# VectorE's attention program written out for all pairs, and a wait for each hidden block ahead of its first down product

## The chip, the cores and the metric

The kernel runs on one core of one Trainium2 chip. The metric is the device time of one execution in microseconds (us), as a median of several runs. Times in the traces are those of one profiled execution.

## The reference

Two layers, each with a token mixer and a mixture of experts, over x of 4 x 1024 tokens with 256 channels. Each layer is x = x + s * silu(m), with both branches taken from the normalised x.

```python
# layer 0: s is a linear-attention-like mixer; m is 16 experts plus a shared one
cap = int(s * 2.0 / 16)                       # 128 tokens for each expert and batch
topk_w, topk_idx = lax.top_k(scores, cap)
g = einsum('becd,efd->becf', x_tok, Wg); u = einsum('becd,efd->becf', x_tok, Wu)
h = gelu(g) * u                               # 512 hidden channels
eo = einsum('becf,edf->becd', h, Wd) * topk_w[..., None]
...
# layer 1: s is causal attention, 16 heads of 64; m is top-2 of 8 experts
sim = einsum('bhid,bhjd->bhij', q * SCALE, k); sim = where(causal_mask, neg, sim)
attn = softmax(sim); out = einsum('bhij,bhjd->bhid', attn, v)
return out.transpose(0, 2, 1, 3).reshape(b, n, INNER) @ Wo
```

The change touches how two of these parts are ordered: layer 0's 16 experts and layer 1's attention. What is computed stays the same.

## The kernel before

The kernel is written with one program for each engine; they wait for each other by semaphores. Its stages, in order of time: normalisation and layer 0's mixer with the shared expert (to about 395 us), the 16 experts (`experts`, about 400 to 762 us) with layer 1's normalisation behind them (`renormalize`, to about 865 us), attention (`attention`, to about 2140 us) and layer 1's experts (`moe`, to the end).

**Experts.** Of each expert, 128 tokens of each of the B = 4 batches are held as 512 columns. TensorE's program of one expert is `expert` (L1026 to L1043): for each of KF = 4 blocks f of 128 hidden channels it makes gate and up (2 products of 128x512 each, L1033); it then transposes the next expert's gathered rows (`follow`, 8 transposes, L1022); and then come the down products (L1040), 4 row blocks b with 4 products each for f = 0 to 3. The listing runs `follow` and then waits for `eo_done` (the last expert's results were read) and for `hid_done` to reach 4 (e + 1): all four hidden blocks of this expert. The trace has two matmuls for each product of the listing (so 32 down matmuls and 32 of gate and up an expert) and one for each transpose. ScalarE makes the gelu of each block (L1064), VectorE multiplies it by the up half and reports it in `hid_done` (L1088), VectorE scales the results (L1093), GpSimd scatters them with addition (L993) and gathers rows for an expert 4 ahead (L973), and SyncE loads the weights two experts ahead once the down products are done (L939 to L941). Experts 0 to 11 run in a loop of 4 on TensorE, experts 12 to 15 are written out.

**Attention.** There are 4 batches (nb) with 8 pairs of heads (PAIRS), 32 pairs in all. TensorE, ScalarE and VectorE each go through one order of events for a pair, written out by hand as PE_ORDER, ACT_ORDER and DVE_ORDER; a "+" marks work of the next pair. Of VectorE's, M is the mask reduction (adds the mask to a piece of scores and takes the running maximum, L1634), I the reciprocal of the sums (L1641), A the copy of v (L1647), P the rotary products (L1654), and W adds a pair's projected output to y (L1669). TensorE's A0, A1, A4, A5 are the query and key products (L1394), A2, A3, A6, A7 the value products (L1400), S the scores (L1409), T transposes (L1417), V the products with v (L1431), W the output projection (L1441). ScalarE's E is the exponential (L1462). GpSimd adds the two halves of the rotary embedding (L1497).

`run` (L1225 to L1243) lays an engine's events out over the pairs. It writes out "first" (the work ahead of pair 0), pairs 0 and 1, then has a loop of two pairs for the rest of batch 0 (L1231), a nested loop of two pairs for batches 1 and 2 (L1234, L1235), a loop of two pairs for the first six of batch 3 (L1239), and pairs 30 and 31 written out. In a loop the values that semaphores are waited for depend on the counter and are worked out with register instructions ahead of the wait. `act_on(part, it, pr, u, seq)` gets the pair's number `it`, its number in the batch `pr`, its parity `u` and its batch `seq`.

Of the kernel before, what the change touches and what calls it, by code (L numbers as in the profile page):

```python
# [26 lines left out]
ONE = 1  # L27
# [3 lines left out]
KF = F0 // P  # L31
# [3 lines left out]
PAIRS = HEADS // 2  # L35
# [875 lines left out]
def experts(nc, d):  # L911


    with ExitStack() as ctx:
# [14 lines left out]
        t_ps, xt_done, ffn_ps, gel_done, hid_done, dn_ps, eo_done = (s.sem(x) for x in ("t_ps", "xt_done", "ffn_ps", "gel_done", "hid_done", "dn_ps", "eo_done"))  # L929
# [5 lines left out]
        with nc.Block() as block:  # L935
# [77 lines left out]
            @block.tensor  # L1013
            def _(pe):
                def turn(i, q):

                    e = i * AHEAD + q
                    pe.wait_ge(gathered[q], 16 * B * (i + 1))
                    pe.wait_ge(xt_done, KC * e + ONE)
                    for c in range(KC):  # L1020
                        for b in range(B):
                            last = pe.transpose(ps[c][:, b * P:(b + 1) * P], xg[q][:, b * C + c * P:b * C + (c + 1) * P], ident[:, :])  # L1022
                        last.then_inc(t_ps, 1)

                def expert(i, q, follow):
                    e, u = i * AHEAD + q, q % 2  # L1026
                    pe.wait_ge(xt_done, KC * (e + 1) + ONE)
                    pe.wait_ge(w_in[u], 48 * (i * 2 + q // 2 + 1) + ONE)
                    for f in range(KF):
                        pe.wait_ge(hid_done, KF * e + max(f - 1, 0) + ONE)  # L1030
                        for w, bank in ((wg[u], ps[2 + 2 * (f % 2)]), (wu[u], ps[3 + 2 * (f % 2)])):
                            for k in range(KC):
                                last = pe.matmul(bank, w[:, k * F0 + f * P:k * F0 + (f + 1) * P], xT[u][k][:, :], start=k == 0, stop=k == KC - 1)  # L1033
                        last.then_inc(ffn_ps, 1)
                    follow()
                    pe.wait_ge(eo_done, B * e + ONE)
                    pe.wait_ge(hid_done, KF * (e + 1) + ONE)
                    for b in range(B):
                        for f in range(KF):
                            last = pe.matmul(ps[6 + b // 2][:, (b % 2) * C:(b % 2 + 1) * C], hid[f][:, b * P:(b + 1) * P],  # L1040
                                             wd[u][:, f * C:(f + 1) * C], start=f == 0, stop=f == KF - 1)
                        if b % 2:
                            last.then_inc(dn_ps, 1)  # L1043

                turn(0, 0)
                with pe.Fori(0, ROUNDS - 1) as i:
                    for q in range(AHEAD):
                        expert(i, q, lambda: turn(i + (q + 1) // AHEAD, (q + 1) % AHEAD))
                for q in range(AHEAD - 1):
                    expert(ROUNDS - 1, q, lambda: turn(ROUNDS - 1, q + 1))  # L1050
                expert(ROUNDS - 1, AHEAD - 1, lambda: None)
                then["tensor"](pe)

# [106 lines left out]
def attention(nc, d, name, b0, nb, scatter):  # L1160

    with ExitStack() as ctx:
# [16 lines left out]
        def scratch(cols):  # L1179
            nonlocal at  # L1180
            at += cols
            return d.moe_w2[:, at - cols:at]

        before, bias, rank, tile_no = d.at_route
        sc, bi, w_r, tmp, slot, both, tot, run_, line = d.sc, *(scratch(W) for i in range(8))
# [39 lines left out]
        def run(eng, act_on):  # L1225

            act_on("first", -1, -1, 1, -1)
            if nb > 1:
                for u in range(2):
                    act_on("both", u, u, u, 0)  # L1230
                with eng.Fori(1, PAIRS // 2) as i:  # L1231
                    for u in range(2):
                        act_on("both", i * 2 + u, i * 2 + u, u, 0)
                with eng.Fori(1, nb - 1) as b:  # L1234
                    with eng.Fori(0, PAIRS // 2) as i:  # L1235
                        for u in range(2):
                            act_on("both", b * PAIRS + (i * 2 + u), i * 2 + u, u, b)
            it = (nb - 1) * PAIRS
            with eng.Fori(0, PAIRS // 2 - 1) as i:  # L1239
                for u in range(2):  # L1240
                    act_on("both", i * 2 + (it + u), i * 2 + u, u, nb - 1)
            act_on("both", it + PAIRS - 2, PAIRS - 2, 0, nb - 1)
            act_on("last", it + PAIRS - 1, PAIRS - 1, 1, nb - 1)  # L1243

        s.start()
        with nc.Block() as block:
# [295 lines left out]
            def _(dve):  # L1542
# [126 lines left out]
                                dve.scalar_tensor_tensor(out=part_y, in0=bank[:, t * C:(t + 1) * C], scalar=inv[:, unit:unit + 1], in1=part_y,  # L1669
                                                         op0=ALU.mult, op1=ALU.add).then_inc(w_added, 1)  # L1670

                run(dve, act_on)
                dve.wait_ge(w_added, nb * (16 * PAIRS) + 16 + ONE)


# [399 lines left out]
```

## Time and profile before

| | us |
| --- | --- |
| median of 3 runs (2583.3 to 2585.82) | 2585.6 |
| the profiled execution | 2586.59 |
| its span in the trace | 2584.8 |
| TensorE busy (matmul) | 2430.4 |
| VectorE busy | 1330.7 |
| ScalarE busy | 1104.8 |
| GpSimd busy | 554.0 |

The profile comes from one execution. PE is TensorE, PEld its weight loads, DVE is VectorE, ACT is ScalarE, POOL is GpSimd, SP is SyncE, which issues most DMAs. Instructions of an engine's sequencer (waits, register work, branches) are not counted as busy. An idle time is put down to the engine whose instruction ended it; "issue" stands where the profile shows no such instruction. The chain of waits that the page follows back from the end stays in the last stage, which the change does not touch, so it is of no use here. The granted clock of TensorE was 1.00 in the stages that the change touches, apart from short stretches.

### The profile page before, as it was taken

The numbers are of one execution on the slowest core, as the hardware profiler recorded it, in microseconds if no ns is written. First come the engines' busy times: TensorE is split into PE (matmuls) and PEld (weight loads), VectorE is DVE, ScalarE is ACT, GpSimd is POOL, SyncE is SP. The second block draws the span as 40 slices with busy tenths as digits, with TensorE's granted clock in tenths as the row PEclk, the third lists the DMA queues.
The fourth block names the chain that finished last, engine by engine and source line by source line (L and its number), as shares of the span: only waits on it lengthen the run. The fifth ranks groups of instructions, "written<-read, shape, count | busy, mean of one in ns | idle before, by whom it ended". The sixth has DMA issues, their size and how long they took to land. (4 is left out here: it accounts for less than half of the span.)

```text
span 2584.8 us, 47040 instructions
## 1 busy us (share of the span) xinstructions
PE 2430.4 (94%) x14584; PEld 1699.0 (66%) x14585; DVE 1330.7 (51%) x3699; ACT 1104.8 (43%) x2581; POOL 554.0 (21%) x510
## 2 busy tenths in 40 slices
PE   6999998999975899999999999999999999999993
PEld 5555555555545566666666666666666668999992
DVE  6766241221217866666666656666666653333334
ACT  3211111111115466666656666566666662222222
POOL 3002001444426233332111111111111101111113
PEclk9999998999998999999999999999999999999996
DMA  6013103865436323332111121111211116666696
GB/s 209 17 49 114 49 17 115 260 209 158 114 71 223 89 88 103 96 91 74 42 41 41 49 57 41 41 41 49 72 54 47 51 52 233 243 236 237 240 340 225
DMA packets 145386, 295.90 MB, mean 114 GB/s; under 512 B 16768, under 2 KB 102288, under 8 KB 134896
## 3 DMA queue, kind: packets, MB, share of 16 engines
q1 hardware_dynamic: 124320, 251.59, 30.4%
q0 software_dynamic: 20944, 42.94, 6.1%
q8 instruction: 45, 0.74, 0.1%
q14 instruction: 77, 0.63, 0.1%
HBM read 193.80 MB, written 67.12 MB: 101 GB/s over the span
## 5 line engine op out<-in xcount | busy, mean ns | idle before, releaser
L1462 ACT ACTIVATE at_p<-at_p,at_nmax 128x640 f32<-128x640 f32 (+7 forms) x512 | 392.8, 768 | 209.2 <-DVE at_nmax L1634 205.8
L1634 DVE CUSTOM_DVE_ANT_0 at_p<-at_ps,atk_mask 128x512 f32<-128x512 f32 (+3 forms) x512 | 282.9, 585 | 174.6 <-PE at_ps L1409 152.7
L1497 POOL TENSOR_TENSOR kept_big<-kept_xg 128x1024 f32<-128x1024 f32 x64 | 150.9, 2358 | 998.3 <-DVE kept_xg L1654 998.3
L1469 ACT ACTIVATE at_pT<-at_ps 128x512 f32<-128x512 f32 (+1 forms) x640 | 311.2, 574 | 100.9 <-PE at_ps L1417 100.8
L1417 PEld LDWEIGHTS at_ps<-kept_ident,at_p 128*128 128x128 f32 x2304 | 256.0, 141 | 117.9 <-issue 62.7
L1417 PE MATMUL at_ps<-kept_ident,at_p 128*128 128x128 f32 x2304 | 304.6, 277 | 15.6 <-ACT at_p L1462 15.0
L1409 PE MATMUL at_ps<-kept_big 64*128 64x512 f32 (+3 forms) x1536 | 297.2, 505 | 5.1 <-DVE at_nmax L1634 2.6
L1431 PE MATMUL at_ps<-at_pT,at_v 128*64 128x256 f32 (+1 forms) x2560 | 270.2, 362 | 1.2 <-issue 1.2
L1669 DVE SCALAR_TENSOR_TENSOR kept_big<-at_ps,at_inv,kept_big 128x256 f32<-128x256 f32 x512 | 213.9, 475 | 79.2 <-PE at_ps L1441 73.5
L1431 PEld LDWEIGHTS at_ps<-at_pT,at_v 128*64 128x64 f32 x2560 | 173.6, 137 | 115.4 <-issue 35.1
L1394 PE MATMUL at_ps<-atk_h,atk_w 128*128 128x512 f32 x512 | 238.1, 598 | 6.5 <-SPq L1256 6.5
L1033 PE MATMUL ex_ps<-kept_big 128*128 128x512 f32 x512 | 225.4, 599 | 0.9 <-ACT kept_big L1059 0.9
L1807 PEld LDWEIGHTS moe_ps<-moe_xT,moe_w 128*128 128x128 f32 x1696 | 197.6, 192 | 3.4 <-ACT moe_xT L1840 0.7
L1807 PE MATMUL moe_ps<-moe_xT,moe_w 128*128 128x128 f32 x1696 | 198.0, 275 | 0.5 <-ACT moe_xT L1840 0.5
L1409 PEld LDWEIGHTS at_ps<-kept_big 64*128 64x128 f32 x1536 | 128.1, 188 | 77.0 <-issue 39.7
L1033 PEld LDWEIGHTS ex_ps<-kept_big 128*128 128x128 f32 x512 | 98.3, 192 | 118.7 <-issue 117.9
L1064 ACT ACTIVATE kept_big<-ex_ps 128x512 f32<-128x512 f32 x64 | 38.2, 597 | 299.9 <-PE ex_ps L1033 299.9
L1782 POOL DMA_INDIRECT z_rows<-moe_yo,moe_to x71 | 68.8, 969 | 376.7 <-DVE moe_yo L1873 376.7
L1394 PEld LDWEIGHTS at_ps<-atk_h,atk_w 128*128 128x128 f32 x512 | 91.1, 193 | 85.3 <-issue 78.5
L1634 DVE CUSTOM_DVE_ANT_0 at_p<-at_ps,atk_mask,at_nmax 128x128 f32<-128x128 f32 (+3 forms) x256 | 134.9, 546 | 20.7 <-PE at_ps L1409 20.7
L1654 DVE TENSOR_TENSOR kept_xg<-kept_xg,atk_cos 128x1024 f32<-128x1024 f32 x64 | 78.1, 1220 | 128.3 <-DMA kept_xg<-kept_xg 128.3
L1088 DVE TENSOR_TENSOR kept_big<-kept_big,ex_ps 128x512 f32<-128x512 f32 x64 | 44.1, 689 | 185.6 <-ACT kept_big L1064 185.6
(236 smaller groups left out, 3349.0 us busy)
## 6 DMA issues: line engine op xcount, KB each, us to landing
moe_w<-in_w_w SPq DMA_DIRECT2D x53, 1028.0 KB, 4.8
kept_xg<-kept_xg SPq DMA_DIRECT2D x256, 128.0 KB, 2.4
atk_first_w<-in_w_w SPq DMA_DIRECT2D x18, 1028.0 KB, 4.8
atk_w<-in_w_qkv SPq DMA_DIRECT2D x32, 384.0 KB, 3.0
slot_in<-kept_big SPq DMA_DIRECT2D x9, 1032.0 KB
kept_big<-in_w_eg SPq DMA_DIRECT2D x16, 512.0 KB, 3.5
kept_big<-in_w_eu SPq DMA_DIRECT2D x16, 512.0 KB, 5.0
kept_big<-in_w_ed SPq DMA_DIRECT2D x16, 512.0 KB, 6.8
```

The source lines that it names most:

```text
L1033: last = pe.matmul(bank, w[:, k * F0 + f * P:k * F0 + (f + 1) * P], xT[u][k][:, :], start=k == 0, stop=k == KC - 1)
L1394: last = pe.matmul(banks[0], w[x][:, k * QKV + m * P:k * QKV + (m + 1) * P], h[:, k * T + half * CH:k * T + (half + 1) * CH], start=k == 0 ...
L1409: pe.matmul(banks[e][:, 0:to - at], qkT[x][e * DH:(e + 1) * DH, n * P:(n + 1) * P], qkT[x][e * DH:(e + 1) * DH, T + at:T + to], start=True ...
L1417: last = pe.transpose(banks[0][:, (i - 4 * j) * P:(i - 4 * j + 1) * P], p[(2 * t + e) % LAG][:, k * P:(k + 1) * P], ident[:, :])
L1431: last = pe.matmul(banks[0][e * DH:(e + 1) * DH, skip:QW], v[x][:, (k * 2 + e) * DH:(k * 2 + e + 1) * DH], pT[n][:, at + skip:at + QW], st ...
L1462: act.activation(buf, buf, ACT.Exp, bias=nmax[:, unit:unit + 1], scale=-1.0, accum_out=rsum[:, unit:unit + 1]).then_inc(exp_done, 1)
L1469: act.activation(dst, ring[RING_BANK[part][ev]][:, 0:(i1 - i0) * P].rearrange("p (k c) -> p k c", c=P), ACT.Copy).then_inc(t_read, 1)
L1497: pool.tensor_tensor(out=qkT[x][:, :].rearrange("p (m t) -> p m t", m=2)[:, :, half * CH:(half + 1) * CH], in0=raw[half][:, :].rearrange(" ...
L1634: ins = dve.tensor_tensor_reduce(out=p[unit % LAG][:, at:to], in0=ring[RING_BANK[part]["S", ((t, c), e), ahead]][:, 0:to - at], in1=mask[: ...
L1654: dve.tensor_tensor(out=both, in0=both, in1=table[:, half * CH:(half + 1) * CH].unsqueeze(1).to_broadcast([P, 2, CH]), op=ALU.mult).then_i ...
L1669: dve.scalar_tensor_tensor(out=part_y, in0=bank[:, t * C:(t + 1) * C], scalar=inv[:, unit:unit + 1], in1=part_y, op0=ALU.mult, op1=ALU.add ...
L1807: last = pe.matmul(bank[:, m * P:(m + 1) * P], w1[q][:, at:at + P], xT[u][:, k * P:(k + 1) * P], start=k == 0, stop=k == KC - 1)
```

## The change

TensorE, in `expert`: in place of one wait for all four hidden blocks ahead of the down products, the first row block (b = 0) waits ahead of each product f for block f alone. The other three row blocks have no wait. VectorE, in `attention`: `run(dve, act_on)` is replaced by "first" and a Python loop over all 32 pairs, so that each pair is written out with constants, and there is no loop on VectorE. Order and content of its events are the same. The programs of the other engines in attention still come from `run`.

```diff
--- before.py
+++ after.py
@@ -1034,9 +1034,10 @@
                         last.then_inc(ffn_ps, 1)
                     follow()
                     pe.wait_ge(eo_done, B * e + ONE)
-                    pe.wait_ge(hid_done, KF * (e + 1) + ONE)
                     for b in range(B):
                         for f in range(KF):
+                            if b == 0:
+                                pe.wait_ge(hid_done, KF * e + f + 1 + ONE)
                             last = pe.matmul(ps[6 + b // 2][:, (b % 2) * C:(b % 2 + 1) * C], hid[f][:, b * P:(b + 1) * P],
                                              wd[u][:, f * C:(f + 1) * C], start=f == 0, stop=f == KF - 1)
                         if b % 2:
@@ -1669,7 +1670,10 @@
                                 dve.scalar_tensor_tensor(out=part_y, in0=bank[:, t * C:(t + 1) * C], scalar=inv[:, unit:unit + 1], in1=part_y,
                                                          op0=ALU.mult, op1=ALU.add).then_inc(w_added, 1)
 
-                run(dve, act_on)
+                pairs = nb * PAIRS
+                act_on("first", -1, -1, 1, -1)
+                for it in range(pairs):
+                    act_on("both" if it < pairs - 1 else "last", it, it % PAIRS, it % 2, it // PAIRS)
                 dve.wait_ge(w_added, nb * (16 * PAIRS) + 16 + ONE)
```

## Rows read from the trace of the kernel before

**Rows 1.** The page: the engines' busy times.

```profile
PE 2430.4 (94%) x14584; PEld 1699.0 (66%) x14585; DVE 1330.7 (51%) x3699; ACT 1104.8 (43%) x2581; POOL 554.0 (21%) x510
```

**Rows 2.** Stages: us, busy us (instructions) of PE PEld DVE ACT POOL, granted clock, DMA share, GB/s.

```profile
900.00:1190.00 290.00, 290.00 (x2058) 196.54 (x2056) 185.98 (x557) 185.77 (x443) 104.23 (x97) 1.00 0.32 96
1190.00:1840.00 650.00, 640.45 (x4535) 432.26 (x4534) 410.89 (x1235) 410.23 (x969) 83.67 (x37) 1.00 0.18 47
1840.00:2060.00 220.00, 220.00 (x1574) 149.94 (x1574) 142.19 (x422) 141.73 (x336) 28.24 (x12) 1.00 0.20 53
```

**Rows 3.** VectorE's mask reductions as a group, 1190:1840, then 1840:2062.

```profile
L1634 DVE CUSTOM_DVE_ANT_0 at_p<-at_ps,atk_mask 128x512 f32<-128x512 f32 (+3 forms) x259 | 143.5, 586 | 103.4 <-PE at_ps L1409 83.4 <-issue 18.9
...
L1634 DVE CUSTOM_DVE_ANT_0 at_p<-at_ps,atk_mask 128x512 f32<-128x512 f32 (+3 forms) x88 | 48.2, 579 | 25.2 <-PE at_ps L1409 24.8
```

**Rows 4.** VectorE's timeline, a turn of the nested loop: start, length, idle before in brackets.

```profile
1257.59 3.23 DVE L1669 SCALAR_TENSOR_TENSOR kept_big<-at_ps,at_inv,kept_big 128x256 f32<-128x256 f32 x8 [1.89 <-PE at_ps L1441]
1263.48 0.56 DVE L1634 CUSTOM_DVE_ANT_0 at_p<-at_ps,atk_mask 128x384 f32<-128x384 f32 x1 [2.66 <-issue]
```

**Rows 5.** VectorE's timeline, a turn of the plain loop.

```profile
1103.41 0.56 DVE L1634 CUSTOM_DVE_ANT_0 at_p<-at_ps,atk_mask 128x384 f32<-128x384 f32 x1
```

**Rows 6.** Instruction packets of queue 14, in 880:1010, 1025:1190 and 1190:1840.

```profile
q14 instruction: 7, 0.06, 0.1%
...
q14 instruction: 1, 0.01, 0.0%
...
q14 instruction: 40, 0.33, 0.2%
```

**Rows 7.** TensorE's timeline behind the late mask reduction.

```profile
1267.42 1.09 PE L1417 MATMUL at_ps<-kept_ident,at_p 128*128 128x128 f32 x8 [1.02 <-ACT at_p L1462]
```

**Rows 8.** TensorE's timeline: where four of the pairs begin their query products.

```profile
906.35 0.59 PE L1394 MATMUL at_ps<-atk_h,atk_w 128*128 128x512 f32 x1
...
945.69 0.59 PE L1394 MATMUL at_ps<-atk_h,atk_w 128*128 128x512 f32 x1
...
1221.12 1.45 PE L1394 MATMUL at_ps<-atk_h,atk_w 128*128 128x512 f32 x3
...
1825.74 1.02 PE L1394 MATMUL at_ps<-atk_h,atk_w 128*128 128x512 f32 x2
```

**Rows 9.** TensorE's timeline, the fifth expert.

```profile
497.71 10.03 PE L1033 MATMUL ex_ps<-kept_big 128*128 128x512 f32 x23
507.58 1.04 PE L1022 MATMUL ex_ps<-kept_ident,kept_xg 128*128 128x128 f32 x8
509.15 7.17 PE L1040 MATMUL ex_ps<-kept_big 128*128 128x256 f32 x32 [0.53 <-DVE kept_big L1088]
```

**Rows 10.** VectorE's timeline in the same expert: the fourth block.

```profile
508.41 0.69 DVE L1088 TENSOR_TENSOR kept_big<-kept_big,ex_ps 128x512 f32<-128x512 f32 x1 [2.75 <-ACT kept_big L1064]
```

**Rows 11.** TensorE's waits through all experts, 398 to 770 us.

```profile
PE ex_ps L1040 <- DVE kept_big L1088: 9.8, 16, 1.5
```

**Rows 12.** TensorE's timeline: first down matmuls of the fifth, 13th and last expert.

```profile
509.15 1.35 PE L1040 MATMUL ex_ps<-kept_big 128*128 128x256 f32 x5 [0.53 <-DVE kept_big L1088]
...
687.77 1.10 PE L1040 MATMUL ex_ps<-kept_big 128*128 128x256 f32 x4 [0.63 <-DVE kept_big L1088]
...
754.91 1.32 PE L1040 MATMUL ex_ps<-kept_big 128*128 128x256 f32 x5 [1.50 <-DVE kept_big L1088]
```

**Rows 13.** GpSimd's waits, 398 to 765 us.

```profile
POOL z_rows L993 <- DVE ahead_eo L1093: 88.8, 8, 15.2
```

**Rows 14.** DMA issues in the experts, 398:765: KB each, median us to landing.

```profile
kept_big<-in_w_ed SPq DMA_DIRECT2D x14, 512.0 KB, 6.8
```

**Rows 15.** TensorE's timeline after the last expert.

```profile
784.79 0.47 PE L500 MATMUL ex_ps<-kept_ident,kept_big 128*128 128x128 f32 x1 [22.73 <-DVE kept_big L432]
```

**Rows 16.** VectorE's waits without a releaser, 880 to 1190 us.

```profile
DVE kept_big L1669 <- issue: 3.6, 2, 2.0
DVE at_p L1634 <- issue: 0.7, 3, 0.4
```

## The prediction

> **What bounds the kernel now.** I read the page's busy times first: TensorE is busy for 2430.4 of 2584.8 us [rows 1]. A change can pay only where it shortens TensorE's own queue or ends one of its waits, so each half of the change is read in its own stretch.
>
> **Attention.** The busy times by stage show TensorE without a gap from 900 to 1190 us and from 1840 to 2060 us, but 9.55 us short in the 650 us between [rows 2]. That middle stretch holds the pairs of batches 1 and 2, which run in the nested loop. Among VectorE's groups there, idle time that names no other engine stands once: 18.9 us of the mask reduction's idle time; in the same group between 1840 and 2062 us, where the pairs of batch 3 run in a plain loop of the same body, it is absent [rows 3]. VectorE's timeline shows the place: the last additions of the odd pair end at 1260.82 us, and the first mask reduction of the next pair starts at 1263.48, after 2.66 us without a releaser [rows 4]. At 1103.41 us, where batch 0's loop turns, it starts without idle time [rows 5]. The nested loop turns back seven times (three inner turns in each of two batches, and one outer turn), and seven times 2.7 us is 18.9. All three loops hold two pairs, yet only the nested one stops.
>
> What stops it is seen in the instruction packets: queue 14 brought 40 of them in the 650 us of the nested loop and one in the 165 us before [rows 6]. So I read a stop as code fetched again. The Trainium skill (Runtime: NRT & Kernel Launch, Instruction fetch mechanics) says that a taken branch whose target lies outside the buffered pages waits for a fetch; the packets agree, though at 8 KB each (0.33 MB in 40) and not the 16 KiB that it names. It has the crossing of a page in straight code mostly hidden, which is what the forecast takes.
>
> Does TensorE pay? Behind the late mask it waits 1.02 us for ScalarE's exponential [rows 7]. Its starts give the whole price. The query products of a pair begin at 906.35, 945.69 and so on every 39.35 us: (1221.12 - 906.35) / 8 = 39.35, over one pair written out on VectorE and seven looped ones. From 1221.12 to 1825.74 there are 15 pairs in 604.62 us, against 15 x 39.35 = 590.2: **14.4 us lost**, 2.05 a turn [rows 8]. The 9.55 us above are less because a matmul's modelled length covers part of each gap.
>
> **What the change does to attention.** VectorE's loops go. The 32 pairs had 10 written-out bodies and now have 32, so 22 more bodies lie in memory, and register work in front of its waits goes. TensorE, ScalarE, SyncE and GpSimd keep their programs.
> - The seven stops: 7 x 2.05 = 14.4 us, all on TensorE's path.
> - The register work is worth nothing: the pair from 906.35 to 945.69 us is already written out on VectorE and takes the same 39.34 us as the looped ones [rows 8]. Its cover is TensorE's own work; without that it would matter.
> - New fetches of straight code: the stretch from 880 to 1010 us, where pairs 0 and 1 and the first pass of the plain loop run code for the first time, drew 7 packets in 130 us [rows 6], about 2.1 a pair for all that this queue serves, and TensorE kept 39.35 us. I take 0; the other end of the bound is a rival below.
> - After a stop has gone, TensorE itself is next: from 900 to 1190 us it has no gap [rows 2].
>
> **What the change does in the experts.** Each of 16 experts ends its gate and up products, turns the next expert's rows (8 transposes) and then waits for the fourth hidden block. In TensorE's timeline the transposes start at 507.58 and are 0.11 apart, so the eighth starts at 508.35 and a product could follow at 508.46; the first down product starts at 509.15 [rows 9], since VectorE's fourth product runs from 508.41 to 509.10 [rows 10]. The waits sum this as 9.8 us in 16 [rows 11], of which the last expert, without transposes, has 1.50 and the 13th 0.63 [rows 12].
>
> Now the products on blocks 0 to 2 of the first row block may start before the fourth block is there; the third was ready one block earlier, 8 matmuls of 0.43 or 3.4 us. Each product is two matmuls in the trace (32 an expert for 16 in the listing). The 32 take 7.17 us; less 0.38 for the last one's length and 0.1 for the first one's exposed weight load, 31 steps make 0.216 each [rows 9]. The exposed load is read from the first five: 1.35 us, where four steps and one length make 1.24 [rows 12]. Three products are 6 x 0.216 = 1.30 us, more than the 0.64 us from 508.46 to 509.10. So the fourth never waits: an expert gains the whole gap of 0.69 and the 0.11 of the load, 0.80. For the 13th to 15th it is 0.1 more, and for the last one, whose products could start after the last up matmul but whose gap is longer than 1.30, it is 1.30. **12 x 0.80 + 3 x 0.90 + 1.30 = 13.6 us.** Below, the bound is 0; above, this is all the idle time there is.
>
> The added waits, three more an expert, I take at nothing: in the gate and up part a wait on the same semaphore already stands ahead of each block, with a value worked out from the loop counter, and 23 matmuls still take 10.03 us without a gap, 0.43 each [rows 9]. That work is the cover, and here it is 0.22 a matmul. If it is gone, the nearest row is the 13th expert's idle time of 0.63 against 0.53 in the loop [rows 9, 12], so 0.1 a wait, 48 x 0.1 = 4.8 us given back. The Trainium skill (Advanced Engine Details and Errata, Network/Comms) puts the reading of a semaphore at 50 to 100 ns. By estimate that is 2.4 to 4.8 us for the 48 and speaks against this edit; no row shows such a cost where matmuls are queued.
>
> Behind the waiting products stand only down products of the same expert. VectorE's scaling and GpSimd's scatter wait for them and come earlier too. GpSimd idles some 10 us an expert before its scatter (8 waits make 88.8 us) [rows 13] and keeps up with a period of 21.5 instead of 22.3 us. The weights for the expert after next are asked for as the next expert begins and needed a period later; the last of them land in 6.8 us [rows 14]. What follows the last expert hangs on its scatter, its rows read back and normalised: TensorE waits 22.73 us for that [rows 15], so the 13.6 us are handed on whole.
>
> **Sum.** The profiled execution took 2586.6 us (span 2584.8 and 1.8 around it), 1.0 above the median of 2585.6. 2586.6 - 14.4 - 13.6 = 2558.6; against the median, **2557.6 us**.
>
> **Rivals.**
> 1. *The early products gain little*, because added waits hold TensorE's queue up: with nothing gained 2585.6 - 14.4 = 2571.2 us, with 4.8 us given back of the 13.6, 2562.4. For it: their cover halves. Against it: the gate and up part. The skill's 50 to 100 ns would end between 2560.0 and 2562.4.
> 2. *The turn still costs*, since TensorE's and ScalarE's loops turn at the same pairs, or another cause sits there: only the experts pay, 2572.0 us. Against it: both loops also turn in batch 0, at 39.35 us a pair.
> 3. *Slower: straight code stops at the ends of its pages.* A stop at the loop's end costs 2.05 us. If each written-out pair had one such stop ahead of a mask reduction, 31 x 2.05 = 63.6, less 28.0, is 35.6 more: 2621.2 us. It decides from 28.0 / 2.05 = 14 stops on. Against it: in batch 0 VectorE has only 0.7 us of waits without a releaser before mask reductions in 310 us [rows 16], though its first two pairs are written out. It has 3.6 us more before its last additions; a looped pair idles there too, 1.89 us, for TensorE [rows 4], so I take these for TensorE's product.
> 4. *Nothing measurable changes*: another limit (a read-back, a row gather) takes both gains: 2585.6 us.
>
> **How the numbers follow.** The forecast has 0.68, with 2554 to 2561 as its own range; rival 1 has 0.15, rival 2 0.08, rival 3 0.05, rival 4 0.04. The predicted time is the likeliest case's. The range for 8 in 10 takes in the forecast and rival 1, with the runs' spread of 1 to 2 us (2583.3 to 2585.8): 2553 to 2572 us. A measurement can tell about 0.2%, or 5.2 us. Faster by more: 0.68 + 0.15 + 0.08 = 0.91. Within it: 0.04. Slower: 0.05.
>
> **What would show it.** In the profile after, the seven nameless waits of VectorE are gone, and 15 pairs take 590 us from start to start. TensorE's wait before the down products is gone, and each looped expert takes 21.5 us. Instruction packets come steadily. The forecast is wrong if pairs run longer than 39.35 us, if nameless waits stand before mask reductions in many pairs, or if the experts' period stays at 22.3 us.

## The result and the profile after

The changed kernel takes **2559.1 us** (median of 4 runs, 2555.9 to 2560.1) against 2585.0 for the kernel before beside it (4 runs, 2583.3 to 2585.8): a ratio of 0.9896, 95% interval 0.9884 to 0.9907. The forecast of 2557.6 us, its sign and its two gains hold. The profiled execution took 2560.1 us, with a span of 2557.7, so 27.1 us of span have gone. In the listing after, the lines behind L1034 stand one lower: the mask reduction is L1635, the query products are L1395, the down products L1041.

The page's busy times of the changed kernel, to set beside [rows 1]:

```profile
PE 2421.2 (95%) x14584; PEld 1698.3 (66%) x14585; DVE 1328.0 (52%) x3699; ACT 1104.5 (43%) x2581; POOL 553.9 (22%) x510
```

TensorE's timeline after: the query products of six pairs (the stretch that answers to [rows 8]), the first of all ahead of them.

```profile
825.60 1.19 PE L1395 MATMUL at_ps<-atk_h,atk_w 128*128 128x512 f32 x1 [6.56 <-SPq L1257]
...
893.20 0.59 PE L1395 MATMUL at_ps<-atk_h,atk_w 128*128 128x512 f32 x1
...
932.54 0.59 PE L1395 MATMUL at_ps<-atk_h,atk_w 128*128 128x512 f32 x1
...
1168.62 0.59 PE L1395 MATMUL at_ps<-atk_h,atk_w 128*128 128x512 f32 x1
...
1208.59 0.59 PE L1395 MATMUL at_ps<-atk_h,atk_w 128*128 128x512 f32 x1
...
1798.85 0.59 PE L1395 MATMUL at_ps<-atk_h,atk_w 128*128 128x512 f32 x1
...
2034.93 0.59 PE L1395 MATMUL at_ps<-atk_h,atk_w 128*128 128x512 f32 x1
```

From 1208.59 to 1798.85 us there are 15 pairs in 590.26 us, where the kernel before took 604.62 [rows 8]: 14.36 us less. From the third pair on every pair now takes 39.34 to 39.42 us, but for one: 1168.62 to 1208.59 is 39.97. The stages from 893.20 to 2034.93, 1141.73 us, took 1155.47 before (906.35 to 2061.82). The busy times by stage say the same (columns as in [rows 2]):

```profile
887.00:1176.00 289.00, 289.00 (x2052) 196.29 (x2050) 184.16 (x555) 185.53 (x441) 103.72 (x96) 1.00 0.32 95
1176.00:1815.00 639.00, 638.47 (x4547) 433.84 (x4544) 412.35 (x1241) 410.93 (x972) 84.17 (x38) 1.00 0.19 48
1815.00:2033.00 218.00, 218.00 (x1568) 148.81 (x1567) 139.41 (x418) 140.85 (x333) 28.23 (x12) 1.00 0.20 53
```

TensorE is 0.53 us short of full in the middle stage, where it was 9.55 short before [rows 2]. VectorE's timeline at the place of the old stop [rows 4], first addition and first mask reduction of the pair after:

```profile
1245.04 3.23 DVE L1670 SCALAR_TENSOR_TENSOR kept_big<-at_ps,at_inv,kept_big 128x256 f32<-128x256 f32 x8 [2.00 <-issue]
1248.18 0.55 DVE L1635 CUSTOM_DVE_ANT_0 at_p<-at_ps,atk_mask 128x384 f32<-128x384 f32 x1
```

The 2.66 us ahead of the mask reduction are gone. The 2.00 us ahead of the additions are no new stop: in this stage the additions' idle time is 38.2 us in both kernels, but 32.0 of it now stands without a name, where before all of it was put down to TensorE's products. In the same stage the costliest group of mask reductions keeps one nameless wait, and queue 14 brings 15 instruction packets in the 639 us instead of 40 in 650 [rows 3, 6]:

```profile
L1635 DVE CUSTOM_DVE_ANT_0 at_p<-at_ps,atk_mask 128x512 f32<-128x512 f32 (+3 forms) x260 | 143.6, 587 | 72.5 <-PE at_ps L1410 69.5 <-issue 2.3 <-remote 0.6
```

```profile
q14 instruction: 15, 0.12, 0.1%
```

In the experts, TensorE's timeline of one expert after (the stretch that answers to [rows 9]):

```profile
482.78 1.04 PE L1022 MATMUL ex_ps<-kept_ident,kept_xg 128*128 128x128 f32 x8
483.66 7.07 PE L1041 MATMUL ex_ps<-kept_big 128*128 128x256 f32 x32
490.56 10.89 PE L1033 MATMUL ex_ps<-kept_big 128*128 128x512 f32 x25
```

The down products follow the transposes at once, and their 32 matmuls take 7.07 us where they took 7.17. The period is 21.52 us (462.14, 483.66 and 505.17 are three starts in a row). TensorE's waits from 398 to 760 us no longer hold the row of [rows 11]; these two are all that is left:

```profile
PE ex_ps L1022 <- PEq L102: 8.3, 1, 8.3
PE ex_ps L1033 <- ACT kept_big L1060: 0.9, 1, 0.9
```

The whole difference of the spans: the first query products come at 825.60 instead of 839.52 us (-13.92); from there to the third pair it takes 67.60 instead of 66.83 (+0.77); the pairs up to the last one's start -13.74; the rest 522.77 instead of 522.98 (-0.21). The sum is -27.10.

### The profile page after: what moved, and what is told of

Read it like the earlier page. It is cut to its first block and busy times, and to the rows that moved or that the text cites. A ratio compares the mean times of both kernels' runs of the same rounds, so it can differ in the third digit from the quotient of the medians.

```text
span 2557.7 us, 45455 instructions
## 1 busy us (share of the span) xinstructions
PE 2421.2 (95%) x14584; PEld 1698.3 (66%) x14585; DVE 1328.0 (52%) x3699; ACT 1104.5 (43%) x2581; POOL 553.9 (22%) x510
## 5 line engine op out<-in xcount | busy, mean ns | idle before, releaser
L1635 DVE CUSTOM_DVE_ANT_0 at_p<-at_ps,atk_mask 128x512 f32<-128x512 f32 (+3 forms) x512 | 281.8, 585 | 138.2 <-PE at_ps L1410 134.9
L1395 PE MATMUL at_ps<-atk_h,atk_w 128*128 128x512 f32 x512 | 238.0, 598 | 6.6 <-SPq L1257 6.6
L1065 ACT ACTIVATE kept_big<-ex_ps 128x512 f32<-128x512 f32 x64 | 38.2, 597 | 287.6 <-PE ex_ps L1033 276.2
L1635 DVE CUSTOM_DVE_ANT_0 at_p<-at_ps,atk_mask,at_nmax 128x128 f32<-128x128 f32 (+3 forms) x256 | 135.0, 546 | 27.5 <-PE at_ps L1410 27.1
L1395 PEld LDWEIGHTS at_ps<-atk_h,atk_w 128*128 128x128 f32 x512 | 90.8, 192 | 85.3 <-issue 78.5
```

The source lines that it names most:

```text
L1395: last = pe.matmul(banks[0], w[x][:, k * QKV + m * P:k * QKV + (m + 1) * P], h[:, k * T + half * CH:k * T + (half + 1) * CH], start=k == 0 ...
L1635: ins = dve.tensor_tensor_reduce(out=p[unit % LAG][:, at:to], in0=ring[RING_BANK[part]["S", ((t, c), e), ahead]][:, 0:to - at], in1=mask[: ...
```

## The experiments

All were timed beside the kernel before, whose medians lie between 2584.6 and 2584.7 us. A ratio is against it.

**1. The VectorE half alone.** The kernel before with the second hunk of the change:

```diff
-                run(dve, act_on)
+                pairs = nb * PAIRS
+                act_on("first", -1, -1, 1, -1)
+                for it in range(pairs):
+                    act_on("both" if it < pairs - 1 else "last", it, it % PAIRS, it % 2, it // PAIRS)
```

> Half of the change alone: VectorE's attention is written out for all pairs, the experts are as before. My theory (the seven stops at the nested loop's turns are VectorE's, and nothing else sits there): 14.4 us less than before, a ratio of 0.9944, TensorE's pairs 39.35 us from start to start throughout, no idle time of VectorE without a releaser at the old turns. The changed kernel's trace lost 0.6 us in pair 8; if that belongs to the new code it comes again here, and the gain is 13.8. The rival (the turns of TensorE's or ScalarE's own loops cost as much): less than 5 us gained.

Measured: 2573.2 us, ratio 0.9957 (0.9943 to 0.9970). In its trace the pairs from 905.88 to 2047.25 us take 1141.37 us, 14.1 less than before. This half is worth 11.5 us by the medians and 14.3 by the spans of the two profiled executions; the profiled execution of before lay 1.9 us above these runs' median. The expected 14.4 us (0.9944) stand at the edge of the interval, so it is the trace that decides, not the medians. The time outside the span was longer too: 2.3 to 2.5 us in each of these runs, 1.7 to 1.9 in those of the kernel before.

**2. The TensorE half alone.** The kernel before with the first hunk:

```diff
-                    pe.wait_ge(hid_done, KF * (e + 1) + ONE)
...
+                            if b == 0:
+                                pe.wait_ge(hid_done, KF * e + f + 1 + ONE)
```

> The other half alone: the waits for each hidden block in the experts, attention from the loops as before. My theory: 13.6 us less (12 x 0.80 + 3 x 0.90 + 1.30), a ratio of 0.9947, each looped expert 21.52 us, no idle time of TensorE before the down products, and the seven stops of VectorE still there at 2.05 us each. If the two halves shared something (a transfer or a read-back that both meet), the two gains would not add up to the whole 25.9 us; I expect them to, within 1.5 us. The rival that waits cost TensorE something has at most 8.8 us gained.

Measured: 2569.8 us, ratio 0.9945 (0.9932 to 0.9959). VectorE's waits from 1176 to 1815 us, where the nested loop is still there:

```profile
DVE at_p L1635 <- PE at_ps L1410: 89.1, 62, 3.8
...
DVE at_p L1635 <- issue: 19.1, 7, 2.9
```

Seven nameless waits of 19.1 us, as in the kernel before (18.9). So the halves are separate: 11.5 and 14.9 us by the medians, 26.4 together, and the whole change gives 25.9.

**3. Only the first product early.** The changed kernel, whose second product already waits for all four blocks:

```diff
-                            if b == 0:
-                                pe.wait_ge(hid_done, KF * e + f + 1 + ONE)
+                            if b == 0 and f < 2:
+                                pe.wait_ge(hid_done, KF * e + (1, KF)[f] + ONE)
```

> The changed kernel, but only the product on hidden block 0 may start early: ahead of the second product TensorE waits for all four blocks. Theory of the forecast (an expert gains the time that products ahead of the wait fill, up to the whole gap of 0.69 us and 0.11 for the exposed weight load): one product is two matmuls of 0.216 us, so 0.43 us an expert go ahead and the load is exposed again at the second product: 16 x 0.43 = 6.9 us of the 13.9 stay, and the time is 7.0 us above the changed kernel, 19.0 below the kernel before. TensorE then idles about 0.26 us before the second product. The rival that the gain comes from somewhere else than the overlap (from a shorter wait instruction, for instance) expects the changed kernel's time.

Measured: 2565.8 us, ratio 0.9928 (0.9915 to 0.9942), 18.9 us faster than before. TensorE's timeline of one expert in it:

```profile
485.06 7.44 PE L1041 MATMUL ex_ps<-kept_big 128*128 128x256 f32 x32
```

The products start behind the transposes, but stretch over 7.44 us instead of 7.07: the rest of the wait stands inside them. The down products begin every 21.88 us: 0.44 less than the 22.32 before, where 0.43 were expected, and 0.36 more than with the whole change. The gain goes by how much work stands ahead of the last block, as the forecast had it.

**4. Many more waits.** The changed kernel with the wait ahead of all 16 products of an expert instead of the first four, 192 waits more:

```diff
-                            if b == 0:
-                                pe.wait_ge(hid_done, KF * e + f + 1 + ONE)
+                            pe.wait_ge(hid_done, KF * e + f + 1 + ONE)
```

> The changed kernel with a wait for the hidden block ahead of each of the 16 down products of an expert instead of the first 4. All added ones are already fulfilled when they are reached. It is four times the suspected cost: 192 waits more. The forecast took an added wait at nothing behind queued matmuls: the changed kernel's time within 1 us, experts of 21.52 us. The rival of 0.1 us a wait: 19.2 us slower than the changed kernel.

Measured: 2559.5 us, ratio 0.9903 (0.9888 to 0.9918). That is 0.4 us from the changed kernel, inside either one's scatter. From the first expert's first down product to the last expert's it takes 321.86 us in both traces (335.03 in the kernel before), so the 192 waits cost nothing that a trace can show. They are there: the condition on the hidden blocks stands at 240 of the down products' weight loads, where the changed kernel has it at 48. But they are no instructions of their own (both profiles list 45455): each rides on a weight load. Waits of this kind, on a value long reached, carried by a weight load and with matmuls queued, are free on TensorE. What a wait costs as an instruction of its own is not tested here.

**5. ScalarE's program written out as well.** The changed kernel with ScalarE's `run(act, act_on)` replaced in the same manner.

> The changed kernel with ScalarE's attention program written out for all 32 pairs too. In the changed kernel's trace the pair from 1168.62 us took 39.97 us instead of 39.35, with TensorE waiting 0.53 us for ScalarE's exponential, just after ScalarE's program left its first loop and went into new code. If that is ScalarE's code being fetched late, the pair takes 39.35 us here and the time is 0.6 us less. If it was TensorE's or VectorE's, it stays. In either case ScalarE's own turns cost nothing in the other pairs, so no more than 0.7 us is to be had; straight code on two engines that stopped at its block ends would show as longer pairs.

Measured: 2559.1 us, ratio 0.9897 (0.9882 to 0.9913). Nothing is gained and nothing lost, though queue 14 brings 69 packets instead of 57. ScalarE's loops turned at no cost to TensorE. The pair expected at 39.35 us takes 39.35, but so it does in experiments 3 and 4, where ScalarE still loops, so this does not show where the 0.6 us came from.

**6 and 7. Code moved by empty instructions: failed.** The kernel before with 64 (then 128) empty instructions on VectorE ahead of attention's normalisation:

```diff
+        for _ in range(64):
+            dve.nop()
```

> The kernel before with all its loops; 64 instructions that do nothing are put into VectorE's program ahead of layer 1's normalisation, where it idles some 11 us. They move the code of all three attention loops by 64 places. Theory A, where the code lies decides: a loop body of two pairs is some 325 instructions; the code comes in packets of 8 KB, 128 instructions if one has 64 bytes; a body that touches three such blocks stays in the buffer and one that touches four does not. In the kernel before only the nested loop touches four. Moved by half a block it touches three, and the loops of batches 0 and 3 touch four: the stops move from the nested loop (7) to two turns in each of the plain loops (4), at about 1024, 1103, 1904 and 1983 us. The time falls by 3 x 2.05 = 6.2 us. Theory B, nesting or the register work in it causes the stop: seven stops where they were, no change of time.

> The control for the run with 64: another 64 instructions that do nothing stand at the start of the experts' part of VectorE's program, so the attention code is moved by 128 places, a whole block. Theory A: everything lies as before against the blocks, so the seven stops are back in the nested loop and the time is that of the kernel before, within 1 us. Theory B: the same time as well. If the extra instructions themselves cost something, it shows here as a longer time.

Measured: 2586.7 (ratio 1.0007, 0.9998 to 1.0016) and 2585.1 us (1.0003, 0.9994 to 1.0012). Both profiles list 47040 instructions, as many as before: the empty instructions never came into the program. These two are further runs of the kernel before and say nothing on the question, though the 128 case looks as if it had met its expectation.

**8 to 11. Code moved by real instructions.** The filler is now an increment of a semaphore that nobody waits for, `dve.sem_inc(d.pad, 1)`. The listings differ in their number and place alone:

```diff
+    d.pad = s.sem("pad")
...
+        for _ in range(64):
+            dve.sem_inc(d.pad, 1)
```

The question is why the nested loop stopped while the two plain loops, with the same body, didn't. Between two turns the trace lists 324 to 328 instructions of VectorE. By estimate from the order of VectorE's compiled instructions, in blocks of 128, the body of batch 0's loop begins about 1 instruction into a block, the nested one's about 73, and batch 3's about 20. A body of 325 that begins up to 59 into a block touches three blocks, and a later one touches four. The counts in the trace alone put the nested body 71 and batch 3's 143 instructions behind batch 0's, within 4 of these places. Where batch 0's body begins stands in no trace; the runs bound it, since its turns are free with 56 more instructions and stop with 64 more.

> The kernel before with 64 instructions more on VectorE, each an increment of a semaphore that nobody waits for, ahead of attention's normalisation, so that all of its loops' code moves by 64 instructions. Place theory (a loop's turn stops where its body, 325 instructions long, lies unluckily against the 8 KB blocks in which queue 14 brings code): the nested loop's seven stops go, and the plain loops of batch 0 and batch 3, two turns each, stop in their stead near 1024, 1104, 1904 and 1983 us: 3 x 2.05 = 6.2 us faster than before, 2579 us. Nesting theory (the stop belongs to the nested loop's own branches and register work): all seven stops stay where they are, no change, 2585 us.

> The kernel before with 128 instructions more on VectorE ahead of attention's loops (64 at the start of the experts' part, 64 ahead of attention's normalisation): 128 is what one packet of 8 KB holds at 64 bytes each. Both theories: the seven stops of the nested loop stay, the plain loops have none, the time is that of before, 2585 us. If the place matters but not by blocks of 128 instructions, this kernel has another number of stops than seven.

> As the kernel with 64 more instructions, but with 56. Place theory: the nested loop's seven stops go, batch 0's loop just escapes, and the two turns of batch 3's loop stop (near 1904 and 1983 us): 5 x 2.05 = 10.3 us faster than before, 2575 us. Nesting theory: seven stops stay, 2585 us.

> With 112 instructions more (56 at the start of the experts' part, 56 ahead of attention's normalisation). Place theory: the nested loop's seven stops go, batch 3's loop keeps turning without one, and the two turns of batch 0's loop stop (near 1024 and 1104 us): 5 x 2.05 = 10.3 us faster than before, 2575 us. Nesting theory: seven stops stay, 2585 us.

Measured, with the pairs over 39.5 us as TensorE's query products show them, each taken over 39.35:

| instructions more | body begins (batch 0, nested, 3) | turns that stopped | lost in them, us | median, us | ratio |
| --- | --- | --- | --- | --- | --- |
| 0 | 1, 73, 20 | 7 nested | 14.4 | 2584.6 | 1 |
| 56 | 57, 1, 76 | outer nested 1, batch 3's 2 | 6.0 + 3.9 | 2580.0 | 0.9981 (0.9972 to 0.9990) |
| 64 | 65, 9, 84 | batch 0's 2, batch 3's 2 | 4.8 + 3.9 | 2581.0 | 0.9985 (0.9976 to 0.9994) |
| 112 | 113, 57, 4 | batch 0's 2 | 4.6 | 2574.7 | 0.9963 (0.9950 to 0.9977) |
| 128 | 1, 73, 20 | 7 nested | 14.4 | 2585.4 | 1.0000 (0.9991 to 1.0009) |

VectorE's timeline with 64 more, at the first turn of batch 0's loop, which was free before [rows 5]:

```profile
1021.84 2.83 DVE L1672 SCALAR_TENSOR_TENSOR kept_big<-at_ps,at_inv,kept_big 128x256 f32<-128x256 f32 x7
1027.68 0.56 DVE L1637 CUSTOM_DVE_ANT_0 at_p<-at_ps,atk_mask 128x384 f32<-128x384 f32 x1 [3.02 <-issue]
...
```

And in the same trace, at a turn of the nested loop, which stopped before [rows 4]:

```profile
1262.67 2.82 DVE L1672 SCALAR_TENSOR_TENSOR kept_big<-at_ps,at_inv,kept_big 128x256 f32<-128x256 f32 x7
1265.62 0.56 DVE L1637 CUSTOM_DVE_ANT_0 at_p<-at_ps,atk_mask 128x384 f32<-128x384 f32 x1
```

The instruction packets go with it. With 64 more, from 950 to 1180 and from 1240 to 1470 us:

```profile
q14 instruction: 16, 0.13, 0.2%
...
q14 instruction: 2, 0.02, 0.0%
```

With 128 more, the same two stretches:

```profile
q14 instruction: 6, 0.05, 0.1%
...
q14 instruction: 15, 0.12, 0.2%
```

So the nesting is no cause: the nested loop turns freely once its body lies well, and the plain loops stop once theirs lie badly. Which turns stop is as the count of blocks has it in all five cases, with one exception. With 56 more, the expectation had two stops and missed the outer turn at 1496 us, which costs more than any other. The expectation's "5 x 2.05 faster" is 2575 us, and 2580.0 was measured. VectorE's timeline there, and TensorE's wait behind it:

```profile
1502.30 0.56 DVE L1637 CUSTOM_DVE_ANT_0 at_p<-at_ps,atk_mask 128x384 f32<-128x384 f32 x1 [5.39 <-issue]
```

```profile
1502.93 2.08 PE L1403 MATMUL at_ps<-atk_w,atk_h 128*128 128x128 f32 x8 [2.69 <-DVE at_nmax L1637]
```

The outer loop's first instructions (the counters' set-up) come right ahead of the inner body. With the body at the start of a block they lie in the block before, so an outer turn touches four blocks where an inner one touches three. The trace shows the break at that place. VectorE's sequencer branches at 1496.41 us, reaches the set-up at 1499.42 and 1499.50, and the first instruction of the inner body only at 1501.81: two stops, of 2.95 and 2.27 us. Queue 14 brings two packets in that time (1496.5 to 1502.3 us, first line), and one in a stop of the kernel before (1260.2 to 1263.4 us, second line):

```profile
q14 instruction: 2, 0.02, 1.2%
...
q14 instruction: 1, 0.01, 0.7%
```

So the 5.39 us are two fetches, one behind the other. With 64 more, the body at 9, the same outer turn is free.

The size of a packet fits. In the changed kernel's straight code, from 1267.85 to 1797.11 us, twelve packets of queue 14 begin 119 to 135 of VectorE's listed instructions apart, 127.6 on average. Also, the profile's packets of queue 14 hold 8 KB (0.12 MB in 15), and the pattern of stops came back after 128 instructions and not after 64. The Trainium skill (Perfetto Trace Analysis, The 4-stage abstract model) gives an instruction 64 bytes, which makes 128 of them to 8 KB, and the trace agrees.

## Why the prediction was right

- **The seven stops, 14.4 us.** 14.36 us went in the stage, 14.1 in the VectorE half alone by its trace. That the stop is code fetched again was read from packets and is now shown: moving the same code moves the stops and the packets with it. What the prediction left unsaid is why only the nested loop stopped. It is the place of the body against the blocks, not the nesting.
- **Rival 2** (the turn still costs) is out: all 15 pairs there run at 39.35 us while TensorE's and ScalarE's loops still turn.
- **Register work worth nothing, straight code worth nothing.** Pairs take 39.35 us written out or looped. The packets come at 15 in 639 us, about one a pair, below the 2.1 a pair read from [rows 6], where code of other engines came in too. Rival 3's stops, 31 of them, didn't come. The nameless wait of 2.3 us that is left before a mask reduction is no stop: in experiment 4 VectorE waits the same 2.34 us at that place, there for TensorE's scores.
- **The sum had every pair at 39.35 us; one took 39.97.** TensorE waits there for ScalarE's exponential:

```profile
1181.17 0.63 PE L1418 MATMUL at_ps<-kept_ident,at_p 128*128 128x128 f32 x4 [0.53 <-ACT at_p L1463]
```

  ScalarE's timeline a little earlier, first in the changed kernel, then in experiment 4:

```profile
1179.03 0.38 ACT L1482 ACTIVATE at_oT<-at_ps 128x256 f32<-128x256 f32 x1 [3.10 <-PE at_ps L1432]
```

```profile
1177.74 0.38 ACT L1481 ACTIVATE at_oT<-at_ps 128x256 f32<-128x256 f32 x1 [1.70 <-PE at_ps L1431]
```

  ScalarE begins 1.3 us late, with its idle time 1.4 us longer. TensorE is on time until it waits. VectorE is on time at 1178.30 us and 0.7 us late at its next mask reduction, so its lateness came after ScalarE's. That pair takes 39.64 to 40.01 us in this profile, in those of both halves and in the two failed controls, which are the kernel before, and 39.35 in the profile of before and in experiments 3, 4 and 5. So the same program has it at one time and not at another, and the change doesn't bring it. The four experiments that have it (1, 2, 6 and 7) were profiled on one chip and the seven that don't on two others, so it may go with the chip. Its cause stays open.
- **The experts, 13.6 us.** The last down products end at 748.43 instead of 762.06 us, 13.63 earlier; up to the first query products it is 13.92. The period of 21.52 us is the 0.80 less that the sum had.
- **Added waits at nothing.** Experiment 4 put four times as many waits there, and the experts took the same time, to 0.1 us. The estimate by the Trainium skill (Advanced Engine Details and Errata, Network/Comms), 2.4 to 4.8 us for the 48, isn't borne out; for 192 more it would be 9.6 to 19.2 us. Rival 1 falls with it.
- **Handed on whole, less 0.8.** What stands between the experts and the third pair took 67.60 us instead of 66.83. The control with 64 empty instructions, which is the kernel before, has 67.84 there, so this is scatter between executions and no price of the change.
- **The miss.** The forecast of 2557.6 missed by 1.5 us, within the runs' own spread, and the profiled execution by the same 1.5 (2560.1 against 2558.6). Its span is 0.9 above the sum: 0.7 more in attention, nearly all of it the long pair, and 0.8 ahead of the third pair, less 0.3 ahead of the first query products and 0.2 behind the last pair's start. The other 0.6 lie outside the span. The sum took 1.8 us there; the changed kernel has 2.3 to 2.4 in its runs, every run of an experiment with VectorE's program written out has 2.1 to 2.5, and every other run has 1.7 to 1.9. Why is not shown.

## What to carry to other kernels

A loop's turn is free or holds VectorE for about 3 us, by where its body lies; here 1.9 to 2.5 us of that reached TensorE, and more in one case below: look for nameless waits on an engine once per turn, and for instruction packets that come with them. If they are there, write the loop out, or make its body touch fewer blocks of 128 instructions; if they aren't, as with ScalarE's loops here, writing it out buys nothing. Where a product sums over blocks, let each one wait for its own block: such waits were free here, where each rides on a weight load and matmuls are queued, and the early products fill the time until the last block is there.

## What the runs showed that was not expected

- The same loop code turns in 0.3 us or in 2.8 to 3.3 us (from VectorE's branch to the next instruction of its sequencer), by a shift of 56 or 64 instructions. Fillers of 112 instructions alone, with no other edit, made the kernel 9.9 us faster. By the count, no single shift frees all three loops: with bodies at 1, 73 and 20 of 128, a shift of 55 to 58 frees the first two, and 108 to 114 the last two. Fillers between the loops weren't tried.
- A stop that lasts longer costs more than in proportion. 5.39 us on VectorE took 6.0 us from TensorE, where 2.66 took 2.05. TensorE's granted clock in three stretches of 10 us around it (columns as in [rows 2]):

```profile
1490.00:1500.00 10.00, 10.00 (x64) 5.74 (x60) 5.03 (x13) 2.09 (x8) 5.32 (x3) 1.00 0.07 26
1500.00:1510.00 10.00, 7.30 (x33) 5.64 (x34) 2.69 (x10) 5.89 (x15) 0.73 (x1) 0.66 0.49 145
1510.00:1520.00 10.00, 10.00 (x74) 6.69 (x72) 8.53 (x25) 6.22 (x15) 0.24 (x1) 1.00 0.12 27
```

  Its mean was 0.66 in the middle one, so it ran part of it at the lower level of 1.2 GHz, around the end of the wait of 2.69 us and behind it. That is the rest of the 6.0 us. The same 14 transposes of a pair at a granted clock of 1.00, in the changed kernel (first line), and here (second line):

```profile
1172.95 1.69 PE L1418 MATMUL at_ps<-kept_ident,at_p 128*128 128x128 f32 x14
...
1504.80 3.41 PE L1420 MATMUL at_ps<-kept_ident,at_p 128*128 128x128 f32 x14
```

  They took 1.7 us more, the 8 value products ahead of them 2.08 instead of 1.05, and the 12 of the scores behind them 2.67 instead of 2.21. With the wait of 2.69 that makes 5.9 us. Around an ordinary stop, from 1260 to 1270 us in the kernel before, it stayed at 1.00.
